# One fused attention and mixture-of-experts block: setup in row tables, second variance from the first, router behind the forget gates, scatters begun in the setup, experts from pair 4

## What is computed

```python
xn = layernorm(x)                         # (x - m) / sqrt(var + 1e-5)
# attention branch, 16 query heads, 8 key/value heads, 64 wide
qkvg  = xn @ w_attn                       # q, k, v and 8 forget gates
log_g = log_sigmoid(6.906768 + qkvg[..., QKV:])
log_G = cumsum(log_g, axis=time)          # decay
a     = (q.k * scale)**2 * exp(log_G[t] - log_G[s] - rowmax), causal   # q, k rotated
y     = headnorm((a @ v) / sum(a)) * ln_w;  attn = y @ w_proj
# expert branch
h     = layernorm(xn) * ln_g + ln_b       # a second norm of the normalised xn
top2 of h @ Wr over 7 experts; position in the expert = running count of its tokens
xe[expert, position] = h[token]           # scatter, at most 366 a slot table
ye    = (silu(xe @ W1) * (xe @ W3)) @ W2
routed = gate weights * ye[expert, position]   # gather
shared = (silu(h @ W1s) * (h @ W3s)) @ W2s
out   = x + attn + routed + shared
```

## Time and profile before

| | |
|---|---|
| median of 3 runs | 1180.68 us (1180.38 to 1182.2) |
| profiled execution, its own time | 1181.45 us |
| its span, first to last instruction | 1179.7 us |
| PE busy / DVE busy | 1085.6 us (92%) / 927.7 us (79%) |
| ACT busy / POOL busy | 768.3 us (65%) / 678.2 us (57%) |
| first score matmul (start of the main part) | 172.36 us into the span |
| mean granted TensorE clock | 0.984 |

### The profile page before, as it was taken

How to read it: one execution, slowest core, us unless ns; L and a number is a source line. 1 busy time by engine, 2 the same in 40 slices (tenths; PEclk the granted TensorE clock), 3 DMA queues, 4 the chain that set the end, 5 groups by cost and what they waited for, 6 DMA issues and landing times.

```text
span 1179.7 us, 23035 instructions
## 1 busy us (share of the span) xinstructions
PE 1085.6 (92%) x8367; PEld 790.3 (67%) x8367; DVE 927.7 (79%) x2046; ACT 768.3 (65%) x1630; POOL 678.2 (57%) x828
## 2 busy tenths in 40 slices
PE   3998788899999999999999999999999998999894
PEld 2665556566666777676767777777767676767663
DVE  6755856887878787878777787978798899998882
ACT  1323446676777786868687777877776677677751
POOL 0240508898988554554636373736577777877531
PEclk9999999999999999999999999999999999999997
DMA  8000101111111102020201111111111111112100
GB/s 226 1 1 1 31 10 51 38 33 32 30 29 45 44 22 74 19 77 19 68 26 43 36 53 44 53 44 28 36 43 42 53 53 49 53 35 68 35 8 18
DMA packets 40080, 49.33 MB, mean 42 GB/s; under 512 B 5631, under 2 KB 28157, under 8 KB 39968
## 3 DMA queue, kind: packets, MB, share of 16 engines
q1 hardware_dynamic: 35872, 42.33, 12.7%
q0 software_dynamic: 4096, 5.54, 1.7%
HBM read 33.15 MB, written 9.18 MB: 36 GB/s over the span
## 4 chain that ended last, share of the span: by engine, by line
PE 62%; POOL 16%; DVE 12%; issue 8%; ACT 1%; DMA 0%; POOLq 0%; SPq 0%; DVEq 0%; ACTq 0%
PE P L674 15%; PE P L644 15%; PE P L552 5%; POOL xe_d L1406 4%; PE P L605 4%; PE P L621 3%; POOL U L1353 3%; PE P L580 3%; PE P L595 2%; POOL U L1357 2%; POOL U L1399 2%; PE P L487 2%; PE P L490 2%; PE P L499 2%; PE P L587 2%
## 5 line engine op out<-in xcount | busy, mean ns | idle before, releaser
L644 PE MATMUL P<-Qt,Kt 64*128 64x256 f32 (+1 forms) x2560 | 293.9, 368 | 0.6 <-DVE U L1221 0.6
L644 PEld LDWEIGHTS P<-Qt,Kt 64*128 64x128 f32 x2560 | 218.7, 186 | 72.5 <-issue 53.8
L838 ACT ACTIVATE U<-P 128x512 f32<-128x512 f32 x384 | 207.5, 595 | 33.0 <-PE P L644 33.0
L674 PE MATMUL P<-U 128*64 128x256 f32 (+1 forms) x1792 | 195.0, 357 | 0.0
L835 ACT ACTIVATE U<-U 128x384 f32<-128x384 f32 x256 | 122.8, 524 | 70.9 <-DVE U L1221 70.8
L1221 DVE SCALAR_TENSOR_TENSOR U<-P,U 128x384 f32<-128x384 f32 x256 | 128.8, 550 | 49.4 <-PE P L644 42.4
L674 PEld LDWEIGHTS P<-U 128*64 128x64 f32 x1792 | 113.1, 137 | 69.4 <-issue 26.0
L1353 POOL TENSOR_TENSOR U<-U,consts 128x192 f32<-128x192 f32 x136 | 81.6, 623 | 131.1 <-ACT U L768 127.7
L1357 POOL TENSOR_TENSOR U<-U 128x384 f32<-128x384 f32 x128 | 134.3, 1049 | 35.2 <-DVE U L1204 19.3
L1251 DVE SCALAR_TENSOR_TENSOR P<-U,ES,P 128x512 f32<-128x512 f32 x192 | 144.3, 751 | 5.2
L1399 POOL TENSOR_TENSOR U<-U,SM 128x1024 f32<-128x1024 f32 x32 | 74.7, 2335 | 123.9 <-DVE SM L1285 123.7
(11 more groups left out here) (180 smaller groups left out, 2042.4 us busy)
## 6 DMA issues: line engine op xcount, KB each, us to landing
...
```

The source lines that it names most:

```text
L644: mm = te.matmul(bank[:, 256 * n:256 * n + 256 - lo], Kt[u % 2][ki][rows, 128 * j:128 * j + 128], Qt[w // 2][rows, 256 * (w % 2) + lo:256 ...
L674: mm = te.matmul(P[3][64 * hd:64 * hd + 64, c + lo:c + 256], vt, A[s % NA][:, o:o + 256 - lo], start=i == 0 and n == 0, stop=i == m and n ...
L838: s.activation(A[n % NA][:, 512 * hd:512 * hd + 512], P[BANK["score", n, hd]][:, :], ACT.Square, scale=0.125, bias=GUARD).then_inc(a_sq, 1)
```

## The change

Five things change in the code.

1. The setup's ticks become row tables, `PE_FIRST`, `ACT_FIRST`, `DVE_FIRST`, `POOL_FIRST`: a row is (kind, at, by, then, na, nb), item (a, b) stands at `at + by * a + then * b`, and `spread` sorts them. `T0` is 200 and only an origin for the main tables. All engines' setup orders change.
2. The second norm no longer reads xn again: its variance is worked out from the first one's as var / (var + 1e-5), its mean is taken as zero. Eight `bn_stats` and eight `bn_aggr` a batch go, three small operations come.
3. `forget` no longer waits for the router's matmuls, the copy of the logits is a piece of its own, and `route` stands right behind `forget`. Its one-hot table lies in a place of its own (`CHOICE`), so `route` no longer waits for the rows' way to HBM (`s_hd`). Most of the first projections now stand behind it.
4. POOL issues 20 of the 64 scatters at the end of the setup (`EARLY`), the other 44 in the main part, one each 2.5 ticks, up to tick 107.
5. The experts run from pair 4 to pair 16, and the 64 gathers and adds from tick 396 to 627, one each 3.67 ticks. Some entries of the main tables move by up to 5 ticks.

```diff
-T0 = 232
+T0 = 200
-FIRST_EXPERT, LAST_EXPERT = 6, 18
-FIRST = {154: ("proj", 0, 0), 158: ("proj", 0, 1), ...
+FIRST_EXPERT, LAST_EXPERT, EARLY = 4, 16, 20
+PE_FIRST = [("xt", 22.05, 28.59, 3.86, 4, 2), ("gate", 31.42, 28, 1.01, 4, 2), ("ht", 27.34, 28.29, 5.22, 4, 2),
+            ...
-SCATTER_AT = [2 * c for c in range(64)]
+SCATTER_AT = [5 * c // 2 for c in range(64 - EARLY)]
-GATHER_AT = [n for n in range(432, NSTEP) if n % 6 in (0, 2)][:64]
+GATHER_AT = [396 + 11 * c // 3 for c in range(64)]
+def spread(rows):
+    items = [(at + by * a + then * b, o, kind, a, b) for o, (kind, at, by, then, na, nb) in enumerate(rows)
+             for a in range(na) for b in range(nb)]
+    return [(kind, a, b) for _, _, kind, a, b in sorted(items)]
...
+            def norms(b):
...
+                ve.wait_ge(v_rs, 26 * b + 12)
+                v.tensor_tensor(rs2, rs, rs, ALU.mult).then_inc(v_rs, 1)
...
+                normalise(0)
+                ve.wait_ge(v_rs, 26 * b + 13)
+                v.tensor_tensor(var, rs2, mv[:, :, 1], ALU.mult).then_inc(v_rs, 1)
+                normalise(1)
+                ve.wait_ge(v_rs, 26 * b + 14)
+                v.tensor_scalar(var, var, 1e-5, None, ALU.add).then_inc(v_rs, 1)
+                normalise(2)
+                yield
+                for k, _ in enumerate(rsqrt(var, half, tmp, rs2, v_rs, 26 * b + 15)):
+                    if k < 5:
+                        normalise(k + 3)
+                    if k % 2:
                         yield
+                if b == 0:
+                    ...
+                    for k in range(NB):
+                        nm = v.tensor_scalar(hn[:, 128 * k:128 * k + 128], xout[:, 128 * k:128 * k + 128],
+                                             rs2[:, k:k + 1], None, ALU.mult)
+                        if k in (3, 7):
+                            nm.then_inc(v_hn, 1)
...
                 ve.wait_ge(p_gate, 4)
-                ve.wait_ge(p_rt, 4)
...
-                oh_flat = RW[:, 3]
+                oh_flat = CHOICE
-                ve.wait_ge(s_hd, 32)
+                ve.wait_ge(p_rt, 4)
+                v.tensor_copy(l3, P[5][:, 256:512].rearrange("p (k e) -> p k e", e=8)[:, :, 0:NE]).then_inc(v_lg, 1)
+                yield
...
+            for kind, a, b in spread(POOL_FIRST):
+                if kind == "norm":
+                    normalise(a + 1)
+                elif kind == "proj":
+                    rotate(("proj", 0, 4 * a + b))
+                elif kind == "scatter":
+                    scatter(a)
```

459 lines of the change are left out of this document (216 added, 243 removed), and 8 rows, old and new, of tables (ACT_FIRST, PE_FIRST).

## The result

The changed kernel takes 1195.14 us (median of 5 runs, 1189.8 to 1196.7) where the kernel before takes 1182.2 us beside it: ratio 1.0095, 95% interval 1.0069 to 1.0122. I had forecast 1167.5. The profiled execution took 1190.25 us, its span is 1188.5 us; it is the second fastest of the five and 4.9 us under their median, so what is read from its trace is rather too small than too large.

The account below looks back on a forecast made before the run. Bounds: PE in the expert stretch, POOL's scatters before it, DVE's `forget`/`route` chain in the setup. Setup -6, scatters -9, first expert +4, gathers -2 sum to -13: 1181.45 becomes 1168.5, on the median 1167.7, stated as 1167.5 us, range 1159 to 1174.

Parts of the forecast that it names:

- First half of the setup, -2.3: Setup up to 86.3 us: of PE's 7.1 us idle, 3.3 come off and 1.0 goes on; bounds 0 and -5.
- The chain, 29.0 us: Setup, DVE's `forget` and `route` up to PE's total: 29.0 us instead of 46.0, with PE waits of 2.5 and 5.
- Behind the total, 44 + 4.4 + 3.5 = 51.9 us: Setup from PE's total to the first scores: 44 us of PE work, 4.4 of waits, 3.5 for the lower clock.
- the setup's -6: Whole setup: main part starts at 166 us, 6 us earlier than before; bounds 158 and 183.
- They cost nothing: End of the setup: the twenty early scatters fit POOL's idle time and cost 0; 2 if POOL were 5 us later.
- Scatters in the main part, -9: Main part's scatter stage: fewer scatters on POOL gain 7 us over 5.4 pairs, plus 2; bounds 0 and -15.
- First expert, +4: First expert's load: POOL runs 7 us behind, pair 6's decay row comes late, +4 us once; bounds 0 and +9.
- Experts from pair 4 ... : 0: Expert stage: starting experts at pair 4 moves work within a stage where PE is full; 0 us.
- The small moves of the main tables: 0, give or take 2: Main part: shifting some entries of the engines' tables costs 0 us, give or take 2.
- the slower one: Rival: the setup's DVE chain keeps its 46 us, main part starts at 183, total 1184.5 us; chance 0.08.
- the idle-moves-on rival (1177): Rival: in the main part PE waits for `max`, `y`, `fin` across DVE and ACT whatever POOL does; 1177 us, chance 0.16.
- Gathers, -2: Last part, gathers and their DVE adds: fewer per pair over more pairs gain 2 us; between 0 and -6.

Follow-up runs that it names:

- run 1: The changed kernel with no early scatters, all 64 in the main part at ticks 0 to 107; first scores at 158.66 us, total 5 us above the 1189 expected.
- run 16: The setup-only kernel with 11 early scatters for 8, the others at ticks 22 to 126; the three scatters saved bring nothing.
- run 18: The setup-only kernel without early scatters, all 64 at ticks 0 to 126; 11.4 us gained at the last pair against the kernel before.
- 8: The kernel before with only the setup changed and 8 early scatters, main part otherwise as before; 1166.35 us, ratio 0.9859.
- run 6: The changed kernel with 8 early scatters for 20 and the four main tables of before, its experts, scatters and gathers at their new places; ratio 0.995.
- run 10: Kernel of run 6 with the gathers back at their old places from tick 432; 2 us gained by the ratios, 0.9 us left at pair 31.

## Why the prediction was wrong

**First half of the setup, -2.3: right in kind, too small.** `forget` starts at 80.40 us for my 84.5, 6.4 us ahead of the 86.8 that I had started from. PE's idle time fell by 4.4 of these, near my bound; the other 2 I did not take apart.

**The chain, 29.0 us: right.** 107.45 - 80.40 = 27.05 us. The waits that I put at 2.5 and 5 us were 1.56 and 3.35.

**Behind the total, 44 + 4.4 + 3.5 = 51.9 us: right.** In run 1, which has no stall, the total starts at 108.26 us and the first scores at 158.66: 50.4 us. So the setup's -6 was mis-sized. Those first scores stand 7.3 us earlier than my 166: 3.3 by the chain's start (81.20 us in run 1), 1.9 by its length, 1.5 behind the total, 0.6 by rounding.

**"They cost nothing": this step failed, and with it the setup's gain.** I asked of the twenty scatters only whether POOL was free, and POOL was. Issued in one close run, they held up PE's releases: first scores at 173.55 instead of 158.66 us. Against 8 early ones it costs 5.5 us at the end by `n1` and 9.6 by the ratios, as they also relieve the main part. Even without the stall there was no room for them: in run 16 the first mask stands at 161.03 us, and twenty close scatters end at about 165.

**Scatters in the main part, -9: right in kind.** From pair 0 to 4 the changed kernel gains 6.0 us with 44 for 64, and the 58.33 us of pairs 2 and 3 fit my 58.5. But a scatter has no one price: my sum had 0.45 us for each, run 18 against 8 has 0.6 for eight ahead of the first rotations, and run 16 against 8 nothing for three more.

**First expert, +4: right in kind, in part by luck.** ACT waited 4.17 us for the decay row and PE 2.7 us in all, of which 1.91 for the expert's slots and 0.75 behind ACT. That POOL is 7 us behind I had worked out with 1.45 us a tick, which stands in no row; by the earlier trace rows it is 61.13 / 40 = 1.53, and then POOL wouldn't be behind. In the trace the last scatter is issued at 334.40 us and SP's load at 336.53.

**"Experts from pair 4 ... : 0": failed.** The work moves, but isn't all repaid: 9.7 us come in from pair 4 to 6, 2.3 go behind pair 18 (run 6 against 8), and 6 us are for the scatters, which must be issued by tick 107 and so begin at tick 0. I had the price of fewer scatters, and not that of the same scatters in fewer ticks: begun at tick 0 they stand ahead of the first rotations (6.5 us by pair 0), begun at tick 16 they are 1.65 ticks apart and cost 8.8 us from pair 0 to 4, where 2 apart cost 1.6. The two pairs from 18 on, which lose their expert, take 61.36 us for 63.37, since gathers stand there now. Why an expert costs more at pair 4 than it gives back at pair 18 stays open.

**"The small moves of the main tables: 0, give or take 2": failed.** They cost 6.0 or 11.7 us, by the kernel they are put into. I looked at how many and how large the moves were, not at what stood on both sides of each. None of my three rivals had this one, and the slower one had another cause (a long chain); the idle-moves-on rival (1177) had the place right (`max`, `y`, `fin`) and not the cause.

**Gathers, -2:** not seen. By run 10 their new places cost 1 to 2 us.

My 1167.5 lies near the setup-only kernel (1166.35). That is luck: its setup gain was 7 us larger than mine, and it has only 8 early scatters, none of the other moves, and so neither the rest of my -9 nor my +4 and -2.
